# Another order in attention's step on TensorE: turned scores, straight weighing, scores, crosswise weighing, maxima

## What is computed

```python
q, k, v = (to_heads(q), to_heads(k), to_heads(v))         # 2 x 16 heads, 1024 tokens, 64 wide
dots = jnp.einsum('bhid,bhjd->bhij', q, k) * SCALE
m = jax.nn.softmax(dots, axis=-1)
diag = jnp.diagonal(m, axis1=-2, axis2=-1)
mu = diag.mean(axis=-1, keepdims=True)
sd = diag.std(axis=-1, ddof=1, keepdims=True)
keep = jnp.abs((diag - mu) / sd) <= Z_THRESH
valid = keep[..., :, None] & keep[..., None, :]
masked = jnp.where(valid, dots, NEG)
attn = jax.nn.softmax(masked, axis=-1)
out = jnp.einsum('bhij,bhjd->bhid', attn, v)              # then out @ w_out.T + b_out
```

## Time and profile before

| | |
|---|---|
| median of 3 runs | 1904.43 us |
| profiled execution | 1905.04 us, span of its records 1903.5 us |
| mean granted clock of TensorE | 0.985 |
| TensorE matmul busy | 1787.5 us (94%) |
| weight load busy | 1216.9 us (64%) |
| VectorE, ScalarE, GpSimd busy | 1326.4, 1149.2, 1172.5 us |
| attention, first scores to last turned scores | about 734 to 1760 us |

### The profile page before, as it was taken

The page is one execution under the profiler, slowest core; times in us unless marked ns, Lnnn a source line. Parts: engine busy times, 40 slices in busy tenths (PEclk is TensorE's granted clock), DMA queues, the critical chain, the costliest instruction groups (busy, mean ns, idle before and its releaser), DMA issues. The chain is left out here.

```text
span 1903.5 us, 29906 instructions
## 1 busy us (share of the span) xinstructions
PE 1787.5 (94%) x11064; PEld 1216.9 (64%) x11064; DVE 1326.4 (70%) x2493; ACT 1149.2 (60%) x1715; POOL 1172.5 (62%) x660
## 2 busy tenths in 40 slices
PE   8998999888999897899999999999999999999888
PEld 5883444334785663577777777777777777765466
DVE  5627899986335764667677777777777767778676
ACT  6326777853435546666766676767676776653554
POOL 5551767874453551277777676777767777777354
PEclk9999999999999998899999999999999999999999
DMA  2000000000001002221212221221212121200100
GB/s 99 1 1 1 1 0 1 1 0 1 0 1 50 1 7 69 56 65 48 60 47 60 48 60 47 59 61 46 71 36 71 47 60 47 57 24 12 50 6 17
DMA packets 43664, 66.03 MB, mean 35 GB/s; under 512 B 24768, under 2 KB 26176, under 8 KB 43264
## 3 DMA queue, kind: packets, MB, share of 16 engines
q1 hardware_dynamic: 43056, 63.54, 13.1%
q10 hardware_dynamic: 432, 0.59, 0.1%
q0 software_dynamic: 32, 0.00, 0.0%
HBM read 29.05 MB, written 1.24 MB: 16 GB/s over the span
## 5 line engine op out<-in xcount | busy, mean ns | idle before, releaser
L2410 POOL TENSOR_TENSOR at_e_lo<-at_e,at_e_hi 128x1024 fp32r<-128x1024 f32 x256 | 612.9, 2394 | 304.2 <-DVE at_e_hi L2385 297.2
L2167 ACT ACTIVATE at_e<-at_ps,at_dropped 128x1024 f32<-128x1024 f32 x256 | 285.7, 1116 | 216.4 <-PE at_ps L1880 200.6
L2264 DVE CUSTOM_DVE_ANT_0 at_ps<-at_ps,at_mask 128x1024 f32<-128x1024 f32 x256 | 313.4, 1224 | 7.3 <-PE at_ps L2000 4.9
L2159 ACT ACTIVATE at_ps<-at_ps,at_neg_diag 128x1024 f32<-128x1024 f32 x256 | 278.6, 1088 | 49.1 <-DVE at_neg_diag L2255 48.7
L2385 DVE CAST at_e_hi<-at_e 128x1024 fp32r<-128x1024 f32 x256 | 228.3, 892 | 23.6 <-ACT at_e L2167 20.4
L1959 PE MATMUL at_ps<-at_kq,at_qk 64*128 64x512 f32 x768 | 226.3, 403 | 12.3 <-DMA at_kq<-at_qk 10.5
L1960 PE MATMUL at_ps<-at_qk,at_kq 64*128 64x512 f32 x768 | 226.4, 403 | 0.0
L2009 PE MATMUL at_ps<-at_qk,at_kq 64*128 64x512 f32 x768 | 224.7, 399 | 1.6 <-DVE at_row_max L2264 1.1
L1880 PE MATMUL at_pv_ps<-at_e_hi,at_v_hi 64*128 64x512 f32 x980 | 225.6, 453 | 0.3 <-issue 0.2
L2010 PE MATMUL at_ps<-at_kq,at_qk 64*128 64x512 f32 x768 | 224.6, 398 | 0.0
L1056 POOL TENSOR_TENSOR mb_work<-mb_work,mb_c 128x1024 f32<-128x1024 f32 x64 | 151.8, 2372 | 96.5 <-DVE mb_work L1025 94.2
(11 more groups left out here) (392 smaller groups left out, 4162.9 us busy)
## 6 DMA issues: line engine op xcount, KB each, us to landing
at_kq<-at_qk SPq DMA_DIRECT2D x128, 256.0 KB, 3.9
at_mask<-at_mask_dram SPq DMA_DIRECT2D x32, 256.0 KB, 3.7
at_recips<-at_recip_row SPq DMA_DIRECT2D x31, 256.0 KB, 4.5
ffn_h_raw<-in_h SPq DMA_DIRECT2D x2, 1024.0 KB, 7.5
at_head_w_raw<-in_w_qkv SPq DMA_DIRECT2D x32, 64.0 KB, 3.9
x<-in_x SPq DMA_DIRECT2D x4, 256.0 KB, 4.9
moe_gate_in<-in_gate_in SPq DMA_DIRECT2D x2, 512.0 KB, 3.8
moe_up_in<-in_up_in SPq DMA_DIRECT2D x2, 512.0 KB, 4.5
```

The source lines that it names most:

```text
L2159: act.eng.activation(ps[:], ps[:], ACT.Exp, scale=SCALE, bias=m.small["neg_diag"][s][:, blk:blk + 1], accum_out=m.small["sums"][s][:, blk: ...
L2167: act.eng.activation(m.e[e % 2][:], slot("turned_scores", h, blk)[:], ACT.Exp, scale=SCALE, bias=m.small["dropped"][h % SLOTS][:, blk:blk ...
L2264: dve.eng.tensor_tensor_reduce(out=ps[:], in0=ps[:], in1=m.mask[h % 2][:], scale=1.0, scalar=-BIG, op0=ALU.add, op1=ALU.max, accum_out=m.s ...
L2410: pool.eng.tensor_tensor(m.e_lo[e % 3][:], m.e[e % 2][:], m.e_hi[e % 3][:].bitcast(F32), ALU.subtract).then_inc(sem["at_lo"])
```

## The change

In TensorE's step, the straight half of the weighing and the small products now stand ahead of the scores, and the crosswise half behind them; projection, values and output still have their straight parts ahead of the crosswise weighing. The maxima move from between the halves to behind the crosswise half. In steps without both weighing and maxima, they stay where they were. `weigh` now waits once, at its head, for the low half of the exponentials (`at_lo`), in place of a wait for the high half there and for the low half ahead of its last pairs. On VectorE the reads of the small products move ahead of the diagonal; the rest of the variance's chain (`keeps`) stays behind it. The order in which banks are handed out (`attention_slots`) is as it was.

```diff
--- before.py
+++ after.py
@@ -2018,7 +2018,7 @@
         g, i = h // GROUP, h % GROUP
         with_ones = m.v_hi[:, blk, i, :, :].rearrange("p a d -> p (a d)")
         hi, lo = m.e_hi[e % 3], m.e_lo[e % 3]
-        pe.wait_ge(sem["at_hi"], e + 1)
+        pe.wait_ge(sem["at_lo"], e + 1)
         pe.wait_ge(sem["at_v_ones"], 1)
         pe.wait_ge(sem["at_v_lo"], 2 * g + 1 + blk // (BLK // 2))
         if blk == 0 and h:
@@ -2030,7 +2030,6 @@
         banks = [m.pv_ps[:, half] for half in HALF]
         both_rows(banks, with_ones, [hi[:, half] for half in HALF], blk == 0 and not turned, False, turned)
         both_rows([bank[0:HD] for bank in banks], m.v_lo[:, blk, i, :], [hi[:, half] for half in HALF], False, False, turned)
-        pe.wait_ge(sem["at_lo"], e + 1)
         mm = both_rows(banks, with_ones, [lo[:, half] for half in HALF], False, blk == BLK - 1 and turned, turned)
         if turned:
             mm.then_inc(sem["at_pv"])
@@ -2091,8 +2090,8 @@
         apart = bool(weighed and tested)
         if at := due(t, AT_TURNED, BLK):
             turned_scores(*at)
-        if at := due(t, AT_SCORES, BLK):
-            scores(*at)
+        if apart:
+            weigh(*weighed, False)
         if at := due(t, AT_MEAN):
             mean(at[0])
         if at := due(t, AT_SQUARE):
@@ -2101,9 +2100,9 @@
             turn_mask(at[0])
         if at := due(t, AT_SHIFT):
             turn_shift(at[0])
-        if apart:
-            weigh(*weighed, False)
-        if tested:
+        if at := due(t, AT_SCORES, BLK):
+            scores(*at)
+        if tested and not apart:
             best(*tested)
         for turned in (False, True):
             if at := due(t, AT_QK):
@@ -2125,6 +2124,7 @@
                     project_out_alone(h)
             if apart and not turned:
                 weigh(*weighed, True)
+                best(*tested)
         if weighed and not apart:
             weigh_alone(*weighed)
             if weighed == (LAST, BLK - 1):
@@ -2357,19 +2357,20 @@
             else:
                 dve.wait_ge(sem["x_attn"], h // 2)
                 dve.eng.tensor_tensor(c.x[:, cols], c.x[:, cols], slot("out", h)[:], ALU.add).then_inc(sem["x_attn"])
+        if at := due(t, AT_MEAN):
+            negate_mean(at[0])
+        if at := due(t, AT_SQUARE):
+            negate_square(at[0])
+        if at := due(t, AT_MASK):
+            mask_rows(at[0])
+        if at := due(t, AT_SHIFT):
+            shift_rows(at[0])
         if at := due(t, AT_SCORES, BLK):
             diagonal(*at)
         if at := due(t, AT_STATS):
             first_stats(at[0])
-        if at := due(t, AT_MEAN):
-            negate_mean(at[0])
         if at := due(t, AT_SQUARE):
-            negate_square(at[0])
             keeps(at[0])
-        if at := due(t, AT_MASK):
-            mask_rows(at[0])
-        if at := due(t, AT_SHIFT):
-            shift_rows(at[0])
         if (at := due(t, AT_RECIP)) and at[0] == LAST:
             last_norm()
         elif at:
```

## The result

The changed kernel takes 1943.2 us (median of 4 runs, 1942.3 to 1944.5), the kernel before 1904.4 in the same session (4 runs, 1903.1 to 1905.6). The ratio is 1.0204, 95% interval 1.0188 to 1.0219: 2.0% slower, far outside the noise. Forecast were 1939 us and a range of 1914 to 1960. The profiled execution took 1942.3 us, its span is 1941.0 against 1903.5.

The account below looks back on a forecast made before the run. Attention was taken as bound by TensorE. Net loss of 1.07 us a head over 30 head changes (32 us) plus 3 us at the start, on 1905.0, gave 1940, or 1939 us against the median; range 1914 to 1960.

Parts of the forecast that it names:

- the start: Attention's first steps: 7 small products wait bare with scores behind them; 0 to 10 us lost, 3 taken.
- (a): Straight to crosswise half of the weighing, now three pairs between: the wait goes, 5.06 x 0.10 = 0.51 us a head.
- (d): TensorE's maxima waiting behind the shift rows: 0.08 us a head removed.
- (b): Step 6's maxima wait for the low half of q and k (L2239); three pairs later it goes, 0.40 us a head.
- (e): Head's end: next straight half waits for ScalarE's copy of the weighing's banks, behind the sums; 0.98 us late.
- s: Start of the last scores pair of a step, the mark from which the prediction measures times.
- (c): Step 0's scores waiting for the moved q and k: 0.26 us a head, gone behind the wait in (e).
- (f): Small products waiting on VectorE or ScalarE, per head: step 5 0.05, step 1 0.30, step 3 net 0.72, step 2 0.22.
- Sum per head: Added waits less removed ones over a head's eight steps: 2.32 - 1.25 = 1.07 us net loss.
- Faster: Rival: ScalarE copies before the sums and VectorE's passes run sooner, so added waits are smaller; 1888 us, chance 0.05.
- Much slower: Rival: VectorE's casts fall behind GpSimd's passes in steps with small products; 42 us more, 1981 us, chance 0.08.
- Not parted: Rival: the weighing's halves stay joined, the 0.10 wait remains and only the order costs; 1954 us, chance 0.03.

Follow-up runs that it names:

- e4: New order only in steps 3 to 7 of each head, old order elsewhere, the weighing's waits as before the change; 1896.4 us, 0.9945 of the kernel before.
- e9: New order only in steps 3 to 7, with small products behind the scores and their VectorE reads behind the diagonal; 1888.3 us, 0.9920 of the kernel before.
- e5: Changed kernel, but ScalarE copies the weighing's banks ahead of the sums of step 7 instead of behind them; 1933.0 us, 1.0139 of the kernel before.
- e3: New order only in steps 1 to 7 of each head, old order elsewhere, the weighing's waits as before the change; 1914.6 us, 1.0044 of the kernel before.
- e1: Changed kernel with the weighing's wait for the low half back in its old place; 1943.0 us, 1.0194 of the kernel before.
- e8: e4 with the two small denominator operations behind step 2's maxima on VectorE; 1893.2 us, 0.9930 of the kernel before.
- e7: Changed kernel with the two small denominator operations behind step 2's maxima on VectorE; 1943.7 us, 1.0199 of the kernel before.
- e2: Changed kernel with small products behind scores and their reads behind the diagonal in steps without weighing; 1931.7 us, 1.0136 of the kernel before.
- e6: Changed kernel with small products behind the scores and their VectorE reads behind the diagonal in every step; 1901.4 us, 0.9979 of the kernel before.

## Why the prediction was right, and where it was off

The mechanism was right step by step; sizes were off in opposite directions and nearly cancelled, so that the total came within 4 us is luck in part. The loss by heads came out at 26 us instead of 32, that of the start at 11 instead of 3.

- **(a) to (d), what goes.** Confirmed: none of the four waits of the earlier trace rows is left. Step 4, which has no extras, went from 3.32 to 3.22 us: the 0.10 that (a) says. I wrote that plain steps would go from 3.41 to 3.19; the 3.41 of the earlier trace rows holds a small product, so that comparison was loose. On TensorE step 7, which is plain too, went from 3.39 to 3.22. That the gain stands by itself is shown by e4 and e9. But the maxima's wait of (b) had cost TensorE 0.26 us a head and not 0.40: taking 0.14 off the loader's idle time was not enough there.
- **(e), the copy.** Forecast: copy at s + 1.86, straight half at s + 3.03. Found: s + 1.86 and s + 2.97. e5 shows that ScalarE's order makes the wait. But e3 and e5 also show that only 0.15 to 0.30 us of step 0 come back without it: behind it stand the moved q and k, or the sums. The prediction has the first of these in (c), as "gone behind the wait in (e)".
- **(f), step 3.** Forecast: pass at s + 2.27, product at s + 3.71. Found: 2.26 and 3.69. But the net is less than 0.72. By the starts on TensorE the turn is 0.95 late after and was 0.44 late before, not 0.26, which I had read from one head: net 0.51. By the waits TensorE idles (13.9 + 5.1)/24 = 0.79 us a head for it after, and before it already idled 5.4/25 = 0.22, nearly all of it in the one head of four where the values' product of step 2 stands ahead (5.2 us, 6 times). In these six heads it was 0.9 late before and is 0.9 late after. Net 0.57 by this measure.
- **(f), steps 1 and 2.** The loader waits 12.4/25 and 9.0/24, less 0.14: 0.36 and 0.23, against 0.30 and 0.22. The products themselves start 0.25 and 0.10 late: the loader's time less 0.14 says too much here as well.
- **Sum per head.** 0.93 measured against 1.07. The added waits are smaller than forecast, 1.78 instead of 2.22 us for the four large ones, and what is removed is smaller too. Over the head changes: 26 us instead of 32.
- **The moved wait for `at_lo`.** Nothing, as forecast (e1).
- **The start.** This is the mis-sized term: "Each can hold back at most the three scores pairs that ran meanwhile ... 0 to 10 us. I take 3". The runs show 11, above even the upper bound; 8.6 of it comes back with the order alone, and 2.3 only where the clock is higher as well. The step that failed is the bound. It counted how much TensorE work stands behind a waiting product, but what is lost is not TensorE's work: a chain that ran beside the scores was strung into line with them, and a link costs the chain's length, 4.3 or 3.6 us, less the 1.9 or 1.7 of the step before. ScalarE's rows of the start had to be followed in order, as was done for the head change.
- **The rivals.** "Faster" rested on the copy not standing behind the sums: it does. "Much slower" wanted VectorE's casts behind GpSimd's passes. There are such casts in the changed kernel, 1.43 us at 1216.60 for instance: from 860 to 1640 us 44 of the 196 begin under a pass and take 1.50 us on average. The kernel before had 65 of 203, at 1.09 us. And 0.93 us is what a head loses with them all, so they don't add 1.4. "Not parted" fell with the gap of 0.21 between scores and crosswise half.

Left open: how far the wait for the moved q and k can be lowered (projecting one step earlier was not tried), and how much of the start's 11 us is the order's and how much the clock's.

## What to carry to other kernels

When work on a bound engine is put between two halves of an operation, write for every instruction behind it the new time at which it is due, counted from one common mark, and beside it the time at which its data come by the *order* of the engine that makes them: that engines are only 70% busy says nothing about either. Do the same sum once for the filling of the pipeline, where a product placed ahead of the work that fed it turns two parallel streams into one chain. And an order that loses in all places together can win in some of them: taken only in steps 3 to 7, the same change made the kernel 0.5% faster, and with the small products left behind the scores 0.8%. Before counting what the removal of a wait will give, look for what is due just behind it: at the head's change the moved q and k, or the sums, took back most of the copy's 0.92 us.

## What the runs showed of the hardware

- **A tiny VectorE operation can cost a whole GpSimd pass.** `tensor_scalar` on 128 x 8 took 0.16 us (mean of 24) with GpSimd between passes and 1.45 us (mean of 26 in e8; 1.36 for the 24 in e7) when it began during a pass of some 2.4 us, ending 0.03 us after it. The Trainium skill, SBUF — State Buffer, "Who interferes with whom", says that `cast` and `tensor_scalar` may take a port pair shared with GpSimd and that the later one is blocked for the whole of the other's instruction; the trace agrees. The maxima's pass (L2264) was not held: in the changed kernel 37 of them began under a GpSimd pass and took 1.23 us on average, the others the same. A cast of 128 x 1024 is held like the `tensor_scalar`: 44 took 1.50 us instead of 0.68 and ended 0.55 us after the pass.
- **The loader's idle time is not TensorE's, and TensorE's is not the loss either.** In e4 the loader stood (17.5 + 5.5)/26 = 0.88 us a head before the turn of the mask and TensorE's matmuls 0.20. The turn started 0.44 us late, and taking the wait away gave 0.30. A matmul lasts 0.39 us where a pair follows after 0.227, so the first 0.16 us of a late start are hidden under the one before:

```profile
PEld at_ps L1977 <- issue: 17.5, 26, 1.3
PEld at_ps L1977 <- DVE at_row_max L2274: 5.5, 25, 0.2
```

- **The clock is worth microseconds at both ends of attention.** e2 and e3 run the same order up to the first exponential: with a mean granted clock of 0.74 from 734 to 800 us it came 54.5 us after the first diagonal, with 0.79 after 52.2 us.
- **A short transfer inside the chip came quickly enough.** The shift rows, moved by DMA and wanted one small product later, held the loader for 0.22 us in e6, a third of what I had allowed.
